# Midpoint stage of a four-layer graph network on one core: TensorE's block loop written out, three factor columns put beside the last 64 columns of the high part

## What is computed

```python
XW = mobius_matvec(W, X)                       # N x 512
gamma = max(2 / (1 - sum(XW * XW, -1)), 1e-15)
denom = clamp_abs(A @ (gamma - 1))             # one column
nom   = A @ (gamma * XW)                       # 512 columns
alpha = sum(A, -1)                             # one column
two_mean = nom / denom
a_mean = two_mean / (1 + sqrt(max(1 - sum(two_mean ** 2, -1), EPS)))
AXW = mobius_scalar_mul(alpha, a_mean)
return expmap0(relu(logmap0(AXW)))
```

## Time and profile before

| | us |
|---|---|
| median of 3 runs | 2470.59 (2469.89 to 2473.35) |
| the profiled execution | 2470.45 |
| its span | 2468.7 |
| TensorE busy | 2295.4 (93%), 29752 matmuls |
| VectorE busy | 1710.3 (69%) |
| ScalarE busy | 1568.3 (64%) |
| midpoint2's matmuls of A | about 1555 to 1795 |
| instruction queue q8, whole span | 205 packets, 3.36 MB |

### The profile page before, as it was taken

The page is one execution under the profiler, slowest core; times in us unless marked ns, Lnnn a source line. Parts: engine busy times, 40 slices in busy tenths (PEclk is TensorE's granted clock), DMA queues, the critical chain, the costliest instruction groups (busy, mean ns, idle before and its releaser), DMA issues. The chain is left out here.

```text
span 2468.7 us, 70243 instructions
## 1 busy us (share of the span) xinstructions
PE 2295.4 (93%) x29752; PEld 1484.0 (60%) x29752; DVE 1710.3 (69%) x2932; ACT 1568.3 (64%) x2557; POOL 34.8 (1%) x43
## 2 busy tenths in 40 slices
PE   7979999999999778999999968899979989999999
PEld 4535555555555348999999954344457545555554
DVE  5747888888887577899999966722367334456674
ACT  3438888888888469899999948411245344445452
POOL 1200000000000000000000000000000000000000
PEclk9989999999999898999999989999989999999999
DMA  4022222322222642111111134011101233434441
GB/s 173 9 78 65 83 82 83 105 88 82 82 82 84 227 153 52 33 51 51 51 51 51 59 94 142 14 34 35 35 32 68 92 99 100 130 102 116 120 133 36
DMA packets 223862, 200.87 MB, mean 81 GB/s; under 512 B 148392, under 2 KB 181326, under 8 KB 219363
## 3 DMA queue, kind: packets, MB, share of 16 engines
q1 hardware_dynamic: 222002, 189.01, 25.1%
q10 hardware_dynamic: 1584, 7.93, 0.9%
HBM read 145.31 MB, written 51.46 MB: 80 GB/s over the span
## 5 line engine op out<-in xcount | busy, mean ns | idle before, releaser
L1419 ACT ACTIVATE m_above<-m_u,m_nvs 128x1408 fp8e5<-128x1408 f32 x320 | 438.4, 1456 | 7.5 <-DMA m_u<-rows 7.5
L951 PE MATMUL m_acc<-keep_z_hi,m_p_hi 128*128 128x448 f16 x968 | 338.0, 353 | 19.6 <-DVE m_p_lo L835 16.7
L951 PE MATMUL m_acc<-keep_z_hi,m_p_lo 128*128 128x448 f16 x924 | 326.2, 353 | 0.0
L951 PE MATMUL m_acc<-keep_z_lo,m_p_hi 128*128 128x448 f16 x924 | 324.8, 352 | 0.0
L1747 PE MATMUL m_acc<-right_x_all,m_b 128*128 128x64 f16 x3872 | 242.1, 194 | 21.6 <-DVE m_b L1477 18.9
L1747 PE MATMUL m_acc<-right_x_all,m_c 128*128 128x64 f16 x3872 | 240.9, 193 | 7.7 <-DVE m_c L1485 4.2
L1747 PEld LDWEIGHTS m_acc<-right_x_all,m_b 128*128 128x128 fp8e5 x3872 | 233.1, 99 | 19.8 <-DVE m_b L1477 19.5
L1749 PE MATMUL m_acc<-right_x_all,m_b 128*128 128x64 f16 x3872 | 242.2, 194 | 0.2 <-issue 0.2
L1749 PE MATMUL m_acc<-right_x_all,m_c 128*128 128x64 f16 x3872 | 240.7, 193 | 0.4 <-issue 0.4
L1747 PEld LDWEIGHTS m_acc<-right_x_all,m_c 128*128 128x128 fp8e5 x3872 | 230.9, 98 | 8.9 <-DVE m_c L1485 5.1
L1749 PEld LDWEIGHTS m_acc<-right_x_all,m_b 128*128 128x128 fp8e5 x3872 | 232.5, 98 | 3.1 <-issue 3.0
(11 more groups left out here) (388 smaller groups left out, 5724.3 us busy)
## 6 DMA issues: line engine op xcount, KB each, us to landing
m_at<-adjT SPq DMA_DIRECT2D x11, 1408.0 KB, 7.0
m_at<-adjT SPq DMA_DIRECT2D x11, 1280.0 KB
m_u<-rows SPq DMA_DIRECT2D x16, 704.0 KB, 4.1
low<-m_lw SPq DMA_DIRECT2D x32, 256.0 KB, 5.1
at<-edge_at SPq DMA_DIRECT2D x22, 352.0 KB, 3.3
keep_at<-at ACTq DMA_DIRECT2D x11, 704.0 KB, 5.9
keep_at_first<-at SPq DMA_DIRECT2D x22, 352.0 KB, 3.5
p_x_all<-x SPq DMA_DIRECT2D x4, 1536.0 KB, 12.1
```

The costliest lines, as they stand in the source:

```text
L951: return pe.matmul(acc[:, n % 3, s, of], part(m, q, s, low), z[:, m % T, s, of], start=first, stop=last, skip_group_check=True)
L1419: last = act.activation(above[:, q % RA, j - j0], u[:, g % RU], ACT.Relu, bias=nvs[:, g // NB, j:j + 1], scale=STEEP, saturate=False)
```

## The change

- On TensorE the hardware loop goes: `tile(ib, q)` is written out for the blocks 1 to 10. ScalarE and VectorE keep their loops.
- The two incs of half_used at the end of a block and the wait for prod_done ahead of them go. SP waits for half_used = ib ahead of the first half and for prod_done = 2 ib ahead of the second. The two incs by which SP started the count go, too.
- gcol is no tile of its own: xs_hi grows from 512 to 516 elements a row, and the three factor columns lie in columns 512 to 514. `xs_narrow` is columns 448 to 514.
- Each group's matmuls become lo (512 columns), hi (448) and narrow (67: the last 64 of the high part and the three factors), in this order. The narrow one goes to the small bank.
- VectorE makes nom in two pieces: 64 columns from small, 448 from hi, with one more wait and inc.
- The waits of `tile` on TensorE lose the inc of pe_gate, and x_packed is waited for in block 1 alone.

```diff
--- before.py
+++ after.py
@@ -1893,7 +1893,9 @@
         main = kit.ps("main", [2, D])
         small = kit.ps("small", [2, 512])
         hi, lo = tp[:].rearrange("p b k c -> p b (k c)"), main
-        xs_hi, xs_lo, gcol, factor = keep["xs_hi"], keep["xs_lo"], keep["gcol"], keep["factor"]
+        xs_lo, factor = keep["xs_lo"], keep["factor"]
+        xs_hi, gcol, CA = keep["xs_hi"][:, :, 0:D], keep["xs_hi"][:, :, D:D + 3], D - DH
+        xs_narrow = keep["xs_hi"][:, :, CA:D + 3]
         DUOS = T // 2
         y_in, x_in = (kit.sems(" ".join(f"{n}{d}" for d in range(DUOS))) for n in ("y_in", "x_in"))
         at_in = kit.sems("at_in0 at_in1")
@@ -1904,9 +1906,9 @@
             "tp_ready hi_ready lo_made mx_done mx_made msq_made link2 asked2 answered2 co_made xhi_made diff_made xs_made "
             "g_made g_ones")
         (prod_done, half_used, low_made, nom_made, sm_made, acc_free, nsq_made, rel_made, rsq_made, ss_done, link, asked,
-         answered, gate, w_in, w_hi_made, w_lo_made, x_packed, pe_gate) = kit.sems(
+         answered, gate, w_in, w_hi_made, w_lo_made, x_packed, side_made, gate2) = kit.sems(
             "prod_done half_used low_made nom_made sm_made acc_free nsq_made rel_made rsq_made ss_done link asked "
-            "answered gate w_in w_hi_made w_lo_made x_packed pe_gate")
+            "answered gate w_in w_hi_made w_lo_made x_packed side_made gate2")
         early = slice(0, T - 2)
         batches = (slice(0, EA), slice(EA, T))
         x_t, y_t = tiles(dram["x1"]), tiles(dram["y1"])
@@ -1948,11 +1950,12 @@
                 sp.dma_start(w[:], dram["w3"].rearrange("(k p) n -> p k n", p=P)).then_inc(w_in, 16)
 
                 def load(ib, half):
-                    wait_count(sp, half_used, 2 * ib + half + 1, gate)
+                    if half == 0:
+                        wait_count(sp, half_used, ib, gate)
+                    else:
+                        wait_count(sp, prod_done, 2 * ib, gate)
                     sp.dma_start(at_pairs[:, half], dram["at8"][:, half * HJ:(half + 1) * HJ, ds(ib * P, P)]).then_inc(at_in[half], 16)
 
-                for half in range(2):
-                    sp.sem_inc(half_used, 1)
                 load(1, 0)
                 load(1, 1)
                 sp.dma_start(xs_hi[32:32 + LAST, T - 1, :], xs_lo[0:LAST, T - 1, :]).then_inc(x_packed, 16)
@@ -1991,37 +1994,31 @@
                         pe.wait_ge(g_ones, 2)
                     a = at[:, j // HJ, j % HJ, q * P:(q + 1) * P]
                     ends = dict(start=(j == 0), stop=(j == T - 1))
-                    pe.matmul(hi[:, q, :], a, xs_hi[:, j, :], **ends)
                     pe.matmul(lo[:, q, :], a, xs_lo[:, j, :], **ends)
-                    last = pe.matmul(small[:, q, 0:3], a, gcol[:, j, :], **ends)
+                    pe.matmul(hi[:, q, 0:CA], a, xs_hi[:, j, 0:CA], **ends)
+                    last = pe.matmul(small[:, q, 0:DH + 3], a, xs_narrow[:, j, :], **ends)
                     if j == HJ - 1 and q == 1:
                         last.then_inc(half_used, 1)
                     if j == T - 1:
                         last.then_inc(prod_done, 1)
-                        if q == 1:
-                            pe.wait_ge(prod_done, 2)
-                            pe.sem_inc(half_used, 1)
 
                 def tile(ib, q):
-                    wait_count(pe, acc_free, free(2 * ib + q), pe_gate)
+                    pe.wait_ge(acc_free, free(2 * ib + q))
                     for j in range(T):
                         if q == 0 and j % HJ == 0:
-                            wait_count(pe, at_in[j // HJ], ib * 16 + 16, pe_gate)
+                            pe.wait_ge(at_in[j // HJ], ib * 16 + 16)
                         a = at[:, j // HJ, j % HJ, q * P:(q + 1) * P]
                         ends = dict(start=(j == 0), stop=(j == T - 1))
-                        if j == T - 1:
+                        if ib == 1 and j == T - 1:
                             pe.wait_ge(x_packed, 16)
-                        pe.matmul(hi[:, q, :], a, xs_hi[:, j, :], **ends)
                         if j < T - 1:
                             pe.matmul(lo[:, q, :], a, xs_lo[:, j, :], start=(j == 0), stop=(j == T - 2))
-                        last = pe.matmul(small[:, q, 0:3], a, gcol[:, j, :], **ends)
+                        pe.matmul(hi[:, q, 0:CA], a, xs_hi[:, j, 0:CA], **ends)
+                        last = pe.matmul(small[:, q, 0:DH + 3], a, xs_narrow[:, j, :], **ends)
                         if j == HJ - 1 and q == 1:
                             last.then_inc(half_used, 1)
                         if j == T - 1:
                             last.then_inc(prod_done, 1)
-                            if q == 1:
-                                pe.wait_ge(prod_done, 2 * ib + 2)
-                                pe.sem_inc(half_used, 1)
 
                 def first():
                     transpose(0)
@@ -2037,7 +2034,10 @@
                     for j, q in order:
                         first_block(j, q)
 
-                loop_blocks(pe, tile, first, lambda: None)
+                first()
+                for ib in range(1, IB):
+                    for q in range(2):
+                        tile(ib, q)
 
             @block.scalar
             def _(act):
@@ -2193,10 +2193,12 @@
                 def tile(ib, q):
                     t = 2 * ib + q
                     dve.wait_ge(prod_done, t + 1)
-                    dve.tensor_copy(sm[:, :, ds(t, 1)], small[:, q, 0:3].unsqueeze(2)).then_inc(sm_made, 1)
+                    dve.tensor_copy(sm[:, :, ds(t, 1)], small[:, q, DH:DH + 3].unsqueeze(2)).then_inc(sm_made, 1)
                     dve.wait_ge(low_made, t + 1)
                     dve.wait_ge(rsq_made, free(t))
-                    dve.tensor_tensor(nom[:, q, :], hi[:, q, :], lowp[:, q, :], ALU.add).then_inc(nom_made, 1)
+                    dve.tensor_tensor(nom[:, q, CA:D], small[:, q, 0:DH], lowp[:, q, CA:D], ALU.add).then_inc(side_made, 1)
+                    dve.tensor_tensor(nom[:, q, 0:CA], hi[:, q, 0:CA], lowp[:, q, 0:CA], ALU.add).then_inc(nom_made, 1)
+                    wait_count(dve, side_made, t + 1, gate2)
                     dve.wait_ge(nom_made, done(t))
                     dve.wait_ge(sm_made, t + 1)
                     dve.sem_inc(acc_free, 1)
@@ -2989,7 +2991,7 @@
             keep |= {n: kit_right.sb(n, [KC, 2 * D + 1], F16, side="right") for n in ("w3_hi", "w3_lo")}
             with ExitStack() as layer:
                 kit = Kit(nc, layer, "keep2")
-                keep |= {"xs_hi": kit.sb("xs_hi", [T, D], F16), "xs_lo": kit.sb("xs_lo", [T, D], F16), "gcol": kit.sb("gcol", [T, 3], F16),
+                keep |= {"xs_hi": kit.sb("xs_hi", [T, D + 4], F16), "xs_lo": kit.sb("xs_lo", [T, D], F16),
                          "at_first": kit.sb("at_first", [2, T // 2, P], F16)}
                 midpoint2(nc, dram, keep)
             layer = stack.enter_context(ExitStack())
```

## The result

The changed kernel takes 2454.36 us (median of 4 runs, 2452.25 to 2457.88), against 2470.82 for the kernel before on the same footing: a ratio of 0.992, 95% interval 0.9907 to 0.9932. That is 16.5 us less, where 19.8 less than the median was forecast; the time lies in the range, 0.6 us under its upper end. The profiled execution took 2453.71 us with a span of 2451.9 us, 16.7 less than the span before (2468.67 and 2451.93 to the hundredth).

What follows compares the result with a forecast made beforehand. TensorE's matmul starts were taken to bound midpoint2. Block 0 1.0, columns 8.75, block ends 9.36 and last block 0.6 sum to 19.7 us off 2470.45: 2450.7, or 2450.8 for the median, range 2448 to 2455.

Steps and rivals of the forecast that it cites:

- TensorE's pace by start to start: midpoint2's block loop: TensorE sets the pace, 457.1 ns a group plus 1.17 us lost at each of 8 jumps back.
- Splits inside a group: Slots read from the trace: small 27.6 ns, hi and lo 214.8 each; attention0's pair 188.5 + 32.1 ns.
- The columns: Tiles 2 to 19: a group falls from 457.1 to 435 ns, saving 8.75 us (8.2 to 9.2).
- Rival (1): The weight load under the narrow matmul shows and the column gain is gone: 2459.5 us; chance 0.04.
- The block ends: Loop of midpoint2: without PE's own wait the 8 jump gaps go to zero, saving 9.36 us.
- DMA cover: Block starts: loads of the next half still land in time, slack 0.3 to 0.7 us for half 0.
- Block 0: Block 0 and its end: tile 2 starts earlier, saving 1.0 us (0.7 to 1.2).
- The last block: Block 10: VectorE, busy with factors(), sets the end, so only 0.6 us is saved (0.4 to 0.75).
- Clock: Later stages after midpoint2: half-clock stretches may come out longer or shorter, +-2 us with no preferred sign.
- (2): Block starts: the gap stays, with the load of at as its releaser, up to 2460 us; chance 0.04.
- (3): TensorE's written-out code: some 10 more instruction fetches stall it, up to 24.4 us lost, 2475.2 us; chance 0.03.
- (4): Block ends are set by TensorE's own queue, not the wait; only columns and 3 us count: 2459; chance 0.04.

Runs made afterwards that it cites:

- e9: The changed kernel with rows of xs_hi 544 elements (1088 bytes) apart in place of 516 (1032 bytes); 2459.55 us, ratio 0.9928.
- e1: The kernel before with only the new columns (512, 448, 67), keeping the hardware loop and PE's wait for its own matmul; 2465.92 us, ratio 0.9964.
- e4: The changed kernel, written out, with PE's wait for its own last matmul and the inc of half_used put back; 2456.95 us, ratio 0.9931.
- e3: The kernel before, loop and columns kept, without PE's wait for its own last matmul; SP waits for prod_done itself; 2462.08 us, ratio 0.9956.
- e11: The changed kernel with TensorE's hardware loop put back, without the wait for its own matmul; 2453.84 us, ratio 0.9917.
- e8: The changed kernel with the first half of the fp8 tiles released two groups later, its load issued 0.87 us later; 2462.94 us, one run.
- e5: The kernel before, unchanged, run and profiled once more; 2474.82 us, ratio 1.0002.
- e12: The changed kernel with VectorE's factors() ahead of block 10 cut to three small operations; tile 19's last matmul to prep3's first transpose 30.70 us.
- e2: The kernel before with TensorE written out and no wait for its own matmul, old columns (512, 512, 3); 2463.31 us, ratio 0.9959.
- e7: The changed kernel with narrow matmuls starting one column later in attention0 (449) and at column 451 in midpoint2; 2457.74 us, ratio 0.9938.

## Why the prediction was right, and where it wasn't

- **TensorE's pace by start to start.** Right. The account of the earlier trace rows held in every profile, and the sum of the touched part, 19.7, met 19.97. That it met so closely is luck: the columns brought 0.8 us less than forecast and the last block 0.8 more.
- **Splits inside a group.** Some were read a nanosecond off. In the trace the small slot of tile 3 is 26.8 ns and not 27.6 (hi and lo 215.0 each), and attention0's 18 pairs are 189.4 + 30.8 = 220.2 ns and not 188.5 + 32.1. The group of 457.1 ns, on which the sum rests, is right.
- **The columns.** 8.75 was forecast with 8.2 to 9.2; the stretch gives 17.42 - 8 x 1.18 = 8.0, just below the range. A group is 436.7 ns, which is the end worked out from attention0's pair, 436.4, and not 435. I went halfway to attention1's 29.4 ns because of its fp8 tiles. What set the price was where the moving rows start: half of the narrow slots take 30 ns and half 35 (shown under e9), and the cheap half's group, 433.3 ns, lies by the other end, 433.9. In attention0 half of the narrow matmuls start off a multiple of 16 bytes, as here, so its pair was the nearer row.
- **Rival (1), the weight load.** Out. A slot of 32.6 ns carries the load of the next tile, in the loop (e1) as well as written out. By the Trainium skill, TensorE: Matmul & The Clock Gate, the sections on LDWEIGHTS and on weight-path modes, the load would have been an estimated 53 ns; the measurement decides.
- **The block ends.** The amount was right: all ten gaps went, 9.45 us for the 8 jumps. The split of a gap into 0.82 for the wait and 0.35 for the jump failed as a sum: 0.47 for the wait alone (e4), nothing for the jump alone (e3, e11), 1.17 for both. The 0.85 us at the loop's exit had looked like the wait alone. So the written-out form, half of the change's name, brings nothing of its own but some 0.1 to 0.3 us at the loop's entry; e11 has the stretch of the changed kernel with the loop.
- **DMA cover.** Right. The slack of 0.3 to 0.7 us is 0.6 by e8, and the changed kernel never waits for at.
- **Block 0.** Forecast 1.0, measured 1.11. Of that 0.89 is the gap ahead of block 1; the rest is small beside the spread, since block 0 to block 1 took 32.42 us in the first profile of before and 33.48 in e5. The wait for acc_free that I expected, 0.1 to 0.3 us, isn't there: 0.03 us from 1589.82 to 1589.85.
- **The last block.** This step failed: 0.6 forecast with 0.4 to 0.75, 1.44 measured. VectorE's copy did come late, 0.9 us behind TensorE's last matmul instead of the 1.3 forecast (0.2 is the distance when VectorE stands ready, as in e12), but I took tile 20's 3.63 us, and 0.15 for the split, for the price of a tile that finds lowp ready. It had an idle 0.2 us between copy and nom in it; tile 21 took 1778.63 to 1782.04, 3.41 us with the split, and its copy starts 19.73 us after tile 19's last matmul, not 20.22. And a late copy costs little, since the tile that comes in time waits 0.47 us for lowp anyway. e12 puts the loss at 0.14 us. So TensorE sets this end as well: it came 1.70 us earlier (20.49 us after tile 19's last matmul before, 18.79 after), and 0.26 of that were lost behind its last matmul.
- **Clock.** Behind the stage the two profiles differ by 0.2 us, inside the +-2. The size was worked out too small: with half clock counted as 0.5, a mean of 0.83 over 17 us is 5.8 us at half clock and 2.9 us lost, not 1.4. Nothing here put it to the test.
- **Rivals (2), (3), (4).** None came. At the present slack (2) needs a load more than 0.6 us later (e8). For (3), 8 more code packets and no idle time on issue (e2). (4) is out by e3: with the wait gone the gaps were gone.
- **The total.** 3.6 us over the forecast time though the sum was right. The term that was missing is the spread upstream: I took one profile of the kernel before as its time, and the two profiles of it reach block 0 at 1555.55 and 1564.78. The range held a clock term of 2 us but none for this spread, while single runs of the kernel before went from 2470.02 to 2482.34 us beside the experiments. The median landed 0.6 us inside the range and one of its four runs (2457.88) outside: that the total held is in part luck. How far the 16.5 us understate the change, whose touched part brought 20, can't be told from one set of four runs.

## What to carry to other kernels

An engine that waits for its own last instruction to pass a release on stands idle for it, 0.47 us here and 1.17 with the loop's jump behind it; let the one who needs the release wait for that instruction's own semaphore. Do this before writing a hardware loop out: without such a wait at its end the loop's jump was free. And move columns into a matmul that is too short to pay for its slot, and price it by the row that has the same operands, the same order and the same row distance. Look at the slots one by one and not only at their mean: here the mean of 32.6 ns hid two kinds, and the row distance told them apart.

## What the runs showed of the hardware

- At a taken jump of TensorE's hardware loop over 260 matmuls and weight loads the start-to-start distance was 0.03 us, the same as without a jump, where TensorE did not wait for its own completion ahead of it (e3, e11). Right behind such a wait the pair cost 1.17 us, leaving the loop behind such a wait 0.82, and the wait in written-out code 0.47 (e4).
- The narrow matmul's slot depends on where its moving rows start. 67 f16 columns in rows 1032 bytes apart take 30 ns where the row starts at a multiple of 16 bytes from the first one and 35 where it starts 8 bytes off (the changed kernel), and in rows 1088 bytes apart always 30.0 (e9). 64 columns from byte 896 of rows of 1024 bytes take 28.4, 63 columns from byte 898 32.0 (e7). With all rows so placed, part of the gain went to the matmul ahead (lo +1.3 ns in e9).
- The same written-out code of 64-column matmuls took 509.7 to 520.5 us in attention1, with 6.6 to 14.2 us of idle time on issue, from one execution to the next (the idle time in the three profiles shown). At 6 instructions in 437 ns, in midpoint2's written-out blocks, there was none.
